# Graph network on one core: in the first layer, one product of 256 columns a tile in place of two of 128, read by VectorE and then by ScalarE

## The reference

```python
deg = jnp.maximum(segment_sum(1, dst), 1.0)
h = relu(x @ ws0 + (segment_sum(x[src], dst) / deg) @ wn0 + b0)      # 64 -> 128
h = relu(h @ ws1 + (segment_sum(h[src], dst) / deg) @ wn1 + b1)      # 128 -> 128
h = h @ ws2 + ...                                                    # 128 -> 64
```

## Time and profile before

| | us |
|---|---|
| median of 3 runs (lowest, highest) | 5099.02 (5089.89, 5105.0) |
| the profiled execution, its own time | 5097.06 |
| its span | 5095.3 |
| PE busy | 4202.0 (82%) |
| DVE busy | 3265.3 (64%) |
| ACT busy | 2762.0 (54%) |
| POOL busy | 3310.3 (65%) |

### The profile page before, as it was taken

How to read it: one execution, slowest core, us unless ns; L and a number is a source line. 1 busy time by engine, 2 the same in 40 slices (tenths; PEclk the granted TensorE clock), 3 DMA queues, 4 the chain that set the end, 5 groups by cost and what they waited for, 6 DMA issues and landing times. The chain is left out here.

```text
span 5095.3 us, 116107 instructions
## 1 busy us (share of the span) xinstructions
PE 4202.0 (82%) x31493; PEld 3798.6 (75%) x31494; DVE 3265.3 (64%) x6692; ACT 2762.0 (54%) x7100; POOL 3310.3 (65%) x3162
## 2 busy tenths in 40 slices
PE   2999999799997899979997455548888599999997
PEld 1899999799997888879997445536767366666665
DVE  5555555677775788857766566657777355555555
ACT  0566666455544777854443566655666244444444
POOL 2544443478773777747774777747775677777772
PEclk9999999899999999989999766679999799999999
DMA  1778787466665677758876566647777244444442
GB/s 35 214 250 252 252 252 248 173 232 242 231 235 211 224 257 261 259 197 275 279 266 232 162 184 184 190 143 216 224 210 205 74 118 117 117 119 119 119 115 89
DMA packets 490328, 991.07 MB, mean 195 GB/s; under 512 B 156821, under 2 KB 246965, under 8 KB 470968
## 3 DMA queue, kind: packets, MB, share of 16 engines
q1 hardware_dynamic: 389368, 872.44, 50.7%
q0 software_dynamic: 100800, 116.72, 11.4%
HBM read 452.18 MB, written 380.15 MB: 163 GB/s over the span
## 5 line engine op out<-in xcount | busy, mean ns | idle before, releaser
L753 PE MATMUL ps_all<-arena 128*128 x16000 | 2023.1, 286 | 501.8 <-DMA arena<-arena 348.3
L753 PEld LDWEIGHTS ps_all<-arena 128*128 128x128 f32 x16000 | 1989.8, 204 | 549.1 <-issue 545.5
L682 POOL DMA_INDIRECT arena<-n_t,ix_now x784 | 907.8, 1158 | 426.2 <-issue 401.1
L682 POOL DMA_INDIRECT arena<-y_t,ix_now x784 | 808.3, 1031 | 347.6 <-issue 329.6
L1132 ACT ACTIVATE arena<-bytes 128x2048 f32<-128x2048 uint8 (+1 forms) x300 | 475.8, 1618 | 381.9 <-DMA bytes<-pairs_d 215.8
L682 POOL DMA_INDIRECT arena<-x_rows,ix_now x392 | 373.7, 953 | 375.1 <-PE ps_all L753 263.7
L682 POOL DMA_INDIRECT arena<-x_t,ix_now x392 | 403.7, 1030 | 176.8 <-issue 166.4
L1667 PE MATMUL ps_all<-w,tp 128*128 128x128 f32 x4000 | 490.9, 276 | 28.8 <-ACT store_b L1810 28.2
L1667 PEld LDWEIGHTS ps_all<-w,tp 128*128 128x128 f32 x4000 | 477.9, 192 | 47.2 <-issue 38.6
L1097 ACT ACTIVATE bytes<-arena 128x1024 uint8<-128x1024 f32 (+1 forms) x200 | 296.8, 1484 | 242.3 <-DMA pairs_d<-bytes 240.5
L712 DVE TENSOR_TENSOR arena<-iota,window 128x1024 f32<-128x1024 f32 x302 | 363.3, 1219 | 100.8 <-ACT bytes L1097 93.9
(11 more groups left out here) (212 smaller groups left out, 7689.5 us busy)
## 6 DMA issues: line engine op xcount, KB each, us to landing
x_t<-store_a SPq DMA_DIRECT2D x150, 512.0 KB
s_t<-store_a SPq DMA_DIRECT2D x50, 1024.0 KB
n_t<-store_b SPq DMA_DIRECT2D x50, 1024.0 KB
load_a<-s_t SPq DMA_DIRECT2D x50, 1024.0 KB
bytes<-pairs_d SPq DMA_DIRECT2D x100, 512.0 KB
y_t<-store_b SPq DMA_DIRECT2D x100, 512.0 KB
load_b<-x_t SPq DMA_DIRECT2D x100, 512.0 KB
arena<-arena SPq DMA_DIRECT2D x147, 192.0 KB
```

Of the source, the lines that this page charges most:

```text
L682: pool.indirect_dma_start(out=slot_rows(at, W, pitch), out_offset=None, in_=table, in_offset=bass.IndirectOffsetOnAxis(ap=ix_now[:, at:at ...
L753: last = pe.matmul(out(j, 2) if wide else out(j, 1), hot, both(rows) if wide else rows, start=(k == 0), stop=(k == n - 1))
```

## The change

The two weight halves are moved through the array side by side: one product of 256 columns a tile. Its 256 results lie side by side in PSUM, so tiles 0 and 1 fill bank 6 and tiles 2 and 3 fill bank 7. Each reader now reads from both banks; `both_banks()` is a view [128, 4 tiles, 256], of which `own` takes the upper 128 columns of each tile and `neighbours` the lower. VectorE reads first, as before after nmmc. ScalarE's copy waits for s1c in place of nmmc. The wait for s1 in `products` is gone; the wait for n1 is ahead of the first product.

```diff
             def own(c):
                 ve.wait_ge(S(f"nmm{c}"), now(m))
-                V.tensor_tensor(tiles3(store_a[u][:, c * 512:(c + 1) * 512], H), tiles3(ps[7], H), row(b1r, H, CT), ALU.add).then_inc(S(f"s1{c}"), 1)
+                V.tensor_tensor(tiles3(store_a[u][:, c * 512:(c + 1) * 512], H), self.both_banks()[:, :, H:2 * H], row(b1r, H, CT), ALU.add).then_inc(S(f"s1{c}"), 1)
...
             def neighbours(c):
-                act.wait_ge(S(f"nmm{c}"), now(m))
-                A.activation(store_b[u][:, c * 512:(c + 1) * 512], ps[6], ACT.Copy).then_inc(S(f"n1{c}"), 1)
+                act.wait_ge(S(f"s1{c}"), now(m))
+                A.activation(tiles3(store_b[u][:, c * 512:(c + 1) * 512], H), self.both_banks()[:, :, 0:H], ACT.Copy).then_inc(S(f"n1{c}"), 1)
...
             pe.wait_ge(S(f"rel{c}"), now(m))
             former("n1")
-            tile_products(pe, tp[c % 2], w1[:, 0:H], ps[6])
-            former("s1")
-            tile_products(pe, tp[c % 2], w1[:, H:2 * H], ps[7]).then_inc(S(f"nmm{c}"), 1)
+            for r in range(CT):
+                last = pe.matmul(self.both_banks()[:, r, :], tp[c % 2][:, r * P:(r + 1) * P], w1[:, :], start=True, stop=True)
+            last.then_inc(S(f"nmm{c}"), 1)
+
+        def both_banks(self):
+
+            return ps_all[:, 6 * 512:8 * 512].rearrange("p (r w) -> p r w", r=CT)
```

## The result

The changed kernel takes 5140.53 us (median of 5 runs, 5127.43 to 5146.03) against 5099.02 (5 runs, 5089.89 to 5105.00): slower by 0.78%, ratio 1.0078 with a 95% interval of 1.0058 to 1.0099, that is 30 to 50 us. The profiled execution took 5140.53 us, its span is 5138.8.

The account below looks back on a forecast made before the run. The prediction took the pass as a TensorE stream with one hole a block. Chain +0.81 less product savings 3 x 0.05 gave +0.66 us a block, 32.3 over 49, plus 0.73: +33 on the 5099 median, 5132; range 5114 to 5150.

Parts of the forecast that it names:

- rival E: The 256 columns are issued as two instructions of 128, so waits remain without the saving: +40 us, 5140; chance 0.05.
- A: The outcome as summed, +0.66 us a block over the pass: 5132 us; chance 0.78.
- The product: On TensorE, eight products of 256 columns take 1.74 us a chunk instead of 1.79, saving 0.05.
- C: Weight loads set the products' pace, so half the loads take 0.90 us, not 1.79: 55 us faster, 5044; chance 0.04.
- The reads: ScalarE's copy follows VectorE's 0.69 us read plus 0.04 hand-over, 0.73 later; 0.14 to the next product; view free.
- The chain to hidden(1): Work on VectorE and ScalarE from products(2) seen ended to hidden(1): 6.41 us instead of 5.60, +0.81 a block.
- the hole: TensorE's wait before products(3) for ScalarE's copy of chunk 2, forecast to grow from 0.56 us a block to 1.3.
- The two margins: Copies before products(1) and products(2) stay covered by TensorE's other work, with 0.19 and 0.11 us to spare.
- D: Margin before products(2) goes or the new wait meets other ScalarE work: +1.2 to 1.3 a block, about 5160; chance 0.07.
- The sum: Per block +0.81 less 3 x 0.05, +0.66 us; 32.3 us over 49 waits, plus 0.73 for the last copy: +33.
- the later passes only shift: Passes after this one start after a meeting of all engines and were charged no extra time.
- B: The later copy is hidden and only the products' savings count: 10 to 14 us faster, 5087; chance 0.06.

Follow-up runs that it names:

- e1: Kernel before, with only ScalarE's copy made to wait for VectorE's read, products and banks unchanged: 5139.07 us against 5097.86, ratio 1.0082.
- e7: Changed kernel with only each block's second one-hot matrices moved behind take on VectorE: 6312.87 us on a slower chip, ratio 1.0017 to the kernel before.
- e8b: Changed kernel with the readers' order turned round, ScalarE copying first: 6465.12 us on a slower chip, ratio 1.0098 to the kernel before.
- e2: Changed kernel with both one-hot steps of a block moved behind the second own read and take on VectorE: 5141.18 us, ratio 1.0085 to the kernel before.
- e4: Kernel before, with the next block's sums(0) moved ahead of products(3) on TensorE: 5158.69 us, ratio 1.0114.
- e5c: Kernel before, with sums(3) moved between products(2) and products(3), on a faster chip: 5070.52 us against 5098.81, ratio 0.9948.
- e3: Changed kernel with the next block's sums(0) moved ahead of products(3) on TensorE: 5153.40 us, ratio 1.0112 to the kernel before.
- e9: Changed kernel with each read split in two and the readers crossed over banks 6 and 7: 6412.38 us against 6403.62 for the kernel before, ratio 1.0008.
- e5: Kernel before, with sums(3) moved between products(2) and products(3), on the chip of 6304 us: 6313.48 us, ratio 1.0019.
- e5b: Kernel before, with sums(3) moved between products(2) and products(3), on the chip of 6404 us: 6421.71 us, ratio 1.0031.

## Why the prediction was right

The direction, the mechanism and, in the pass, the size hold; 5132 was forecast with 5114 to 5150, 5140.5 was measured. The total alone would fit rival E (5140) better than A; only the trace tells them apart. By its steps:

- **The product**: 1.74 us forecast, 1.72 to 1.73 measured (507.97 to 509.69, 511.62 to 513.35). e1 against the changed kernel prices it by itself: 9.2 us over the pass, 3 x 0.06 x 49 = 8.8. Half as many weight loads brought 0.06 us a chunk, so the loads were hidden. C and B are out. Rival C took its case from a sentence of the Trainium skill (TensorE: Matmul & The Clock Gate, The mechanism), that loads overlap running products only when they go to other row groups. The same section of the Trainium skill also lets a load into a background weight buffer be pulled ahead, and 1.72 to 1.73 us a chunk agree with that, not with the row groups.
- **The reads**: hand-over 0.04 (501.38 after 500.65 + 0.69), restart 0.14 (502.12 after 501.98), both as read from before. No price for the view: 691 ns, and 597 for the copy.
- **The chain to hidden(1)**: 6.41 forecast, 6.38 measured; own(3) at 3.57 forecast, 3.56 measured (504.21). That only 0.1 us of the 0.8 comes from the chain, and the rest from the hole, stood in the sum (6.28 by PE's order); e7's 6.30 and e8b's 6.26 show it.
- **The two margins** held: products(2) of the next turn start at 515.11, behind PE's own order (513.35 + 0.84 for the sums and 0.92 for `hidden(3)`), and no wait is named there. D is out, and E, since the 256 columns came as one instruction.
- **The sum**: period 16.41 by the terms, 16.38 measured; pass +33 forecast, +32.7 measured.

One size is off: the total moved by 41.5 us, the pass by 32.7. The step that doesn't fit is "the later passes only shift". The profiled executions differ by another 10.8 us outside this pass (43.5 us of span less 32.7). In the kernels on the faster chips pass and total agree: +41.9 and +41.2 (e1), +43.9 and +43.3 (e2), +60.3 and +60.8 (e4), -28.1 and -28.3 (e5c), +54.4 and +55.5 (e3). The kernel before alone spreads over 15 us, the changed one over 19, and the interval of 30 to 50 us takes in 33. Nor is there one place where the 10.8 us arise. Against the trace before, the last start of one line in each of five later passes comes 34.5, 35.8, 41.7, 37.9 and 43.5 us later (L1996, L1408, L1500, L1563 and L2315 of before); in e1 these are 46.2, 46.8, 44.6, 41.3 and 42.7. And when pass and span of the same execution are compared, e3 and e4, too, differ outside the pass, by -5.1 and +9.2 us. So scatter in the later passes is the likely cause of the rest; a repeated comparison of this kernel was not made, and it stays open.

## What to carry to other kernels

Before a product is made wider, ask what it does to the readers: two engines that read different banks at once become two that take turns, and here that cost about 0.8 us a block to save 0.06 a chunk. Price a new wait at the place where the waiting engine has the least other work between (here one transpose), and follow what is queued behind it only after that. Splitting each read in two and crossing the readers over the banks (e9) gave the cost back. A hole is filled with work whose inputs have landed for some other reason; work that is first in line for a transfer closes a loop with it (e4, +61 us), work that is last in line does not (e5c, -28 us).

## What the runs showed of the hardware that was not expected

The kernel before took 5098 and 5099 us on the chips of e1 to e4 and of e5c, and 6304 and 6404 us on two others, with a mean granted clock of 0.86 to 0.87 there and 0.93 to 0.94 on the faster ones. An order that wins 0.5% on a faster chip (e5c) loses 0.2 to 0.3% on these (e5, e5b). In this pass the granted clock is little of that (0.98 to 1.00 from 170 to 920 us in all seven runs on these chips); what stands out there are waits that no engine released. Without them, in the last four blocks, these chips run the pass at the faster chips' pace: 15.10 us a block in e5, e5b and e5c. They also turn an order of kernels round: the pass of e7 (848.4 us) is shorter than that of e5 (854.1) on the same chip, though its undisturbed block is 1.2 us longer. What in the transfers is slower on these chips was not looked into.
